# A new order of work for every engine in a four-stage transformer block on one core

## What is computed

```
x = x + tanh(g_xattn[0]) * L0_xattn(ctx, layernorm(x))      # queries from x, keys and values from [ctx | x], 8 heads of 64
x = x + tanh(g_ffn[0])   * L0_ffn(layernorm(x))             # quantised linear, depthwise conv, silu, quantised linear
x = x + tanh(g_xattn[1]) * L1_xattn(layernorm(x), ctx, ctx) # 16 heads of 8, rotary positions, 77 keys
x = x + tanh(g_ffn[1])   * L1_ffn(layernorm(x))             # 8 experts of 64, top 2, and a shared one
```

```
sim  = einsum('bhid,bhjd->bhij', q / scale, k)
attn = softmax(sim - max(sim))
out  = einsum('bhij,bhjd->bhid', attn, v) @ Wout
```

## Time and profile before

| | before |
|---|---|
| time, median of 3 runs | 274.52 us (273.43 to 274.93) |
| span of the profiled execution | 271.8 us |
| TensorE busy | 250.7 us (92%) |
| VectorE busy | 230.8 us (85%) |
| ScalarE busy | 184.1 us (68%) |
| GpSimd busy | 32.4 us (12%) |

### The profile page before, as it was taken

How to read it: one execution, slowest core, us unless ns; L and a number is a source line. 1 busy time by engine, 2 the same in 40 slices (tenths; PEclk the granted TensorE clock), 3 DMA queues, 4 the chain that set the end, 5 groups by cost and what they waited for, 6 DMA issues and landing times.

```text
span 271.8 us, 5455 instructions
## 1 busy us (share of the span) xinstructions
PE 250.7 (92%) x1772; PEld 185.5 (68%) x1772; DVE 230.8 (85%) x561; ACT 184.1 (68%) x462; POOL 32.4 (12%) x57
## 2 busy tenths in 40 slices
...
PEclk9999999999999999999999999999999999999999
...
DMA packets 8848, 10.70 MB, mean 39 GB/s; under 512 B 1115, under 2 KB 5877, under 8 KB 8821
## 3 DMA queue, kind: packets, MB, share of 16 engines
...
q10 hardware_dynamic: 1029, 0.65, 0.8%
...
## 4 chain that ended last, share of the span: by engine, by line
PE 62%; DVE 23%; issue 7%; ACT 6%; DMA 1%; DVEq 0%; ACTq 0%
PE slot L535 18%; PE slot L621 11%; PE slot L602 6%; PE slot L603 5%; PE slot L580 3%; PE slot L762 3%; PE slot L628 2%; PE slot L586 2%; DVE nm L1063 2%; ACT S L916 2%; DVE mx L1172 2%; ACT PR L842 2%; PE slot L756 2%; PE slot L592 1%; PE slot L713 1%
## 5 line engine op out<-in xcount | busy, mean ns | idle before, releaser
L842 ACT ACTIVATE PR<-slot,nm 128x589 f32<-128x589 f32 x64 | 47.6, 750 | 14.8 <-DVE nm L1063 12.5
L1063 DVE TENSOR_REDUCE nm<-slot 128x1 f32<-128x589 f32 x64 | 46.4, 763 | 3.6 <-PE slot L603 3.2
L535 PE MATMUL slot<-K,PR 128*128 128x128 f32 (+1 forms) x320 | 44.4, 278 | 1.7 <-ACT PR L842 1.5
L535 PEld LDWEIGHTS slot<-K,PR 128*128 128x128 f32 (+1 forms) x320 | 35.5, 142 | 12.3 <-ACT PR L842 10.2
L602 PE MATMUL slot<-KH,Q 128*128 128x296 f32 (+1 forms) x128 | 40.7, 336 | 0.8 <-DVE PT L779 0.4
L621 PE MATMUL slot<-PT,V 128*64 128x256 f32 (+1 forms) x320 | 38.1, 384 | 0.0
L603 PE MATMUL slot<-KL,Q 128*128 128x296 f32 (+1 forms) x128 | 36.1, 299 | 0.0
L621 PEld LDWEIGHTS slot<-PT,V 128*64 128x64 f32 (+1 forms) x320 | 21.6, 137 | 11.9 <-issue 2.7
L602 PEld LDWEIGHTS slot<-KH,Q 128*128 128x128 f32 x128 | 24.1, 188 | 5.6 <-issue 2.1
L777 ACT ACTIVATE PT<-slot 128x640 f32<-128x640 f32 x34 | 23.5, 705 | 6.4 <-PE slot L535 5.8
L779 DVE COPY PT<-slot 128x640 f32<-128x640 f32 x30 | 24.4, 820 | 2.6 <-PE slot L535 2.3
(11 more groups left out here) (170 smaller groups left out, 502.2 us busy)
## 6 DMA issues: line engine op xcount, KB each, us to landing
...
out<-X SPq DMA_DIRECT2D x8, 64.0 KB, 1.5
...
```

The costliest lines, as they stand in the source:

```text
L535: return pe.transpose(dst, src, ident[0:p, 0:p])
L842: act.activation(PR[:, s, :], W[:, K0:K0 + KEYS0], ACT.Exp, bias=nm0[:, s:s + 1], accum_out=sum0[:, b, p * 2 + f, t, e:e + 1]).then_inc(pr ...
L1063: dve.tensor_reduce(nm0[:, s:s + 1], W[:, K0:K0 + KEYS0], AX.X, ALU.max, negate=True).then_inc(max_ready, 1)
```

## The change

Only PLAN is replaced; no function changes. The words are the same but for the letters of the copies, and every engine's list has a new order. Of the 64 copies of u, 45 are ScalarE's and 19 VectorE's (34 and 30 before); of the 16 of a4, all 16 are ScalarE's (14 and 2 before); of the eight of f3, four each (six and two before); of the six of v, five are ScalarE's and one VectorE's, as before, but VectorE's is now the first of batch 0 (two chunks of 512 columns) and not the third (one chunk). Banks differ. s stands near the start, behind the first two rows of scores. f4 of tiles 2 and 3 of batch 0 comes before the last w of batch 1, and a4(0,0,0) too. m2 of tile 0 and 1, m3 of part 1 and m4 of tile 0, batch 0, come later against the last a4. The 86 turns stand at 11 places: 6 ahead of the first u, then 8 at the turn of a4(0,0,1), 3 and 7 ahead of f2(1,2) and f2(1,3), 26 and 8 ahead of a4(0,2,0)'s and a4(0,2,1)'s scores, 2, 3, 10, 7 and 6 at f3, a4(0,2,0)'s turn and f4 of batch 1. Behind f4(1,2) there is none. The lines cut here are of the same make.

```diff
 PLAN = """
-x0:F0 x0:A1 k:F2+8@2 x0:D2 q:F4 k:A1 k:F0 q:A1 k:D1 v:F6 x0:P2 k:A1 q:D1 v:F2 v:Ca k:D1 q:F5 v:Ca u:F6 x0:D3
-q:A1 u:F2 u:F0 u:D1 v:F4 u:D1 u:A1 u:D1 u:A1 u:B v:Cd u:A1 u:B u:Cd q:F4 u:Ca q:D1 u:F6 u:F2 u:D1 u:B u:D1
-q:F5 u:A1 u:Cd u:A1 u:B w:D0 s:D2 u:F0 w:P1 u:Ca u:B u:D1 u:F6 u:Ca u:D1 u:A1 u:F2 u:A1 u:B u:D1 q:A1 u:B
...
-f4:A1 u:B w:D0 u:D1 u:A1 w:P1 f4:B f3:F0 u:Cd u:A1 u:B f3:D1 w:F4 u:Ca f4:D2 f3:A1 f3:Ca f4:P2 u:F6 f4:D3
-w:A1 u:F0 w:D1 u:D1 a1:F5 o:F4 a1:A1 u:D1 u:A1 a1:P1 a2:F5 o:D1 u:A1 u:B a2:D1 o:F4 u:Ca u:B w:D0 o:D1 w:P1
...
-a1:A1 a4:A1 a2:F7 a1:P1 f1:D1 a2:D1 f2:F6 a4:A1 a4:B a4:D1 f2:A1 f2:F7 a4:D3 a4:Ca a4:B f2:A1 f2:D1 f2:F2
-f2:F3 a4:Ca f2:A1 a4:F0 f2:D1 f2:A1 f2:A2 f2:D1 a4:F6+8@6 f2:A2 a4:A1 f2:D1 f2:D2 a4:B+10@2 f2:D2 f2:A2
-a4:D1 f2:A2 a4:Ca a4:F2 f2:D2 a4:A1 f2:D2 a4:B+6@4 a4:D1 f3:F4 a4:Ca a4:D1 f3:F5 a4:A1 a4:F0 f3:D1 f3:D1
-f3:A1 a4:B a4:A1 f3:Cd f3:F4 a4:D3 f3:A1 a4:B a4:D3 a4:Ca f4:F5 f3:Ca a6:D0 f3:F6 f3:D1 a6:P1 f4:A1 f4:F7
...
-f4:B a2:D1 a4:B a4:Ca a6:D3 a4:F6+10@4 f4:D2 m1:F4 a4:F0 a4:D1 m1:A1 f4:P2 m3:F2 a4:D1 a4:A1 a4:F4 m3:D1
-a4:A1 f4:D3 a4:B+10@3 a4:D3 m3:A1 a4:B a4:Ca a4:D3 a1:F3 a4:Ca m2:F6 a4:D1 a1:A1 m3:D2 a1:P1 a4:F0 a4:A1
-m2:B a2:F3 a4:D1 m2:A1 a4:B m2:A2 m2:P1 a2:D1 a4:A1 a4:Ca a4:B+7@2 a6:D0 a4:F4 a4:D3 a6:P1 a4:Ca a6:F2 m2:D1
-a6:D0 a4:D1 a4:F0 m2:D2 a6:A1 a6:P1 a4:A1 a6:D1 a4:F6 a4:D1 a6:B a6:F3 a4:D1 a4:A1 a6:D2 a4:A1 a4:B a4:B
-a4:Cd a6:P2 a4:Cd a4:F4+5@2 a6:A1 a6:D3 a4:B a6:D1 m1:F2 a4:D3 a4:Ca m4:F0 a4:D1 a6:B m1:A1 m4:A1 m3:F2
-m2:F6 a6:D2 a4:A1 m4:B m2:A1 m2:P1 a4:D3 a4:B m4:D2 m2:B a6:P2 a6:D0 a4:Ca m3:D1 a6:P1 m2:F0 m2:A2 a6:D3
...
+x0:F4 x0:A1 k:F0 q:F6 k:A1 v:F4 q:A1 k:D1 q:D1 k:F2 k:A1 v:Cd v:F0 u:F6+6@4 v:Ca k:D1 u:F2 u:F4 u:F0 u:D1 u:A1 u:D1 u:B u:D1
+u:A1 u:D1 u:A1 u:B u:B u:Cd u:A1 u:Cd u:F6 u:Ca u:B u:F4 s:D2 u:D1 u:Ca v:F2 u:A1 s:F3 u:D1 s:D1 u:A1 q:F1 v:Ca u:B
+w:D0 u:B u:Ca u:F2 w:P1 k:F6 u:D1 u:Ca u:F4 q:A1 k:A1 q:D1 u:D1 u:A1 k:D1 w:F0 u:B u:A1 w:D0 u:B w:A1 u:Ca u:F6 w:D1
+u:Ca u:F2 u:F0 u:D1 u:A1 u:D1 u:D1 u:F4 u:B u:D1 u:A1 u:B u:A1 u:Cd u:Cd u:A1 u:B u:Cd u:F6 w:D0 u:B q:F2 q:A1 u:F0
...
+u:B u:B u:F2 u:Ca u:D1 f4:A1 a3:F4 f3:Ca w:P1 u:A1 f4:D3 a3:D1 w:F1 f4:B u:Ca f4:D2 u:B w:A1 a3:P1 u:Ca u:F6 w:D1 a1:F0 a1:A1
+u:F4 o:F2 u:D1 u:A1 f4:F1 a2:F3 u:D1 o:D1 u:B u:A1 f4:A1 f4:B w:D0 w:P1 u:Ca u:B o:F2 u:Ca a2:D1 f4:D2 o:D1 f4:P2 a4:F6 a4:D1
+w:F2 w:A1 f4:D3 n:P2 a3:F0 n:D3 w:D1 o:F2 a3:D1 o:D1 o:F5 a4:F2 o:D1 a4:D1 a4:A1 a4:B a4:F0 a4:Ca a4:A1 a1:F7 a1:A1 n:P2 a4:B+8@4 a4:D1
+a4:F6 n:D3 a2:F5 f1:F4 a4:A1 a4:D1 f1:A1 a4:Ca f1:D1 a4:D3 f2:F2 f2:A1 a2:D1 f2:F3 f2:A1 f2:D1 a4:B a4:Ca f2:A2 f2:D1 f2:F5+3@4 f2:D2 f2:F2+7@4 f2:A1
+a4:A1 f2:A1 f2:D1 f2:A2 a4:F4+26@0 a4:B f2:D2 f2:D1 f2:A2 a4:Ca a4:F6+8@0 a4:D1 f2:A2 f2:D2 a3:P1 a4:A1 f2:D2 a1:P1 a4:D1 f3:F2 f3:D1 f3:F1+2@0 f3:F3 a4:A1
+a4:B+3@0 a4:Ca f3:A1 a4:B f3:D1 f3:Cd f3:A1 f4:F4+10@0 f3:F5 f3:D1 f4:A1 f3:Ca f3:D1 f4:B f4:F1 f3:A1 f4:D2 f4:A1 a4:D3 a4:Ca f3:Ca f4:B+7@0 a4:F2 f4:F0
+f3:A1 a1:P1 f4:A1 f4:D2 f4:P2 a4:D1 f4:B+6@1 a1:P1 a6:D0 f4:D3 a4:F4 a6:P1 f3:Ca a4:A1 f4:F7 a1:F1 f4:D2 a6:F6 a4:D1 a1:A1 a2:F0 a4:D3 a4:B a6:A1
+a6:D1 f4:A1 a4:A1 f4:B a4:B a4:Ca a2:D1 f4:D2 a4:F2 a4:D1 a4:F0 f4:P2 a4:Ca a4:A1 a4:D3 a6:B a4:F4 a4:D1 f4:D3 a1:F7 a1:P1 a6:D2 a4:A1 a1:A1
+a4:B a4:Ca a4:D1 a4:B a6:D0 a4:Ca a4:F6 a2:F2 a4:D3 a4:D1 a6:P1 a4:A1 a6:P2 a6:F1 a4:B a6:D3 a4:A1 a4:B a6:A1 m1:F0 a4:Ca m1:A1 a2:D1 a4:D3
+a6:D1 a4:F4 a4:F2 m3:F0 a4:D1 a4:Ca a4:D1 a6:B a6:D0 a4:F6 a4:A1 a4:A1 a6:P1 a4:B a4:Ca a4:B a6:D2 m3:D1 a4:Ca m3:A1 a4:D1 a4:A1 a4:F4 m3:D2
+a6:F2 a6:P2 a6:A1 m2:F0 a4:D1 a6:D1 m2:A1 a6:D3 a4:B m2:B a4:A1 m1:F3 a4:D3 a4:Ca a4:D3 m2:A2 a6:B a4:B a6:D0 m2:F6 m2:P1 m2:D1 a4:Ca m2:B
+m1:A1 a6:P1 m2:A1 a6:D2 m2:A2 m3:F3 m2:D2 m2:P1 a6:F2 m4:F0 m2:F4 m2:D1 m2:B a6:P2 m3:D1 a6:D3 m3:A1 m3:D2 a6:A1 m4:A1 a6:D1 m2:A1 m2:D2 m4:B
...
 """
```

More of the change, by code:

```diff
@@ L107 @@
[L107 to L121, removed]
@@ L127 @@
-u:B u:Ca a3:F2 n:P2 u:Cd n:D3 w:F4 a3:D1 a3:F0 w:A1 w:D1 a3:P1 f4:F5 a3:D1 f4:F6 f4:A1 o:F7 f4:A1 o:F4 o:D1
-a3:P1 f4:B f4:B o:D1 a4:F2 f4:D2 a4:F0 n:P2 f4:D2 a4:F4 n:D3 f4:P2 f4:D3 f1:F6+22@6 a4:D1 a1:F7 f1:A1 a4:D1
-a1:A1 a4:A1 a2:F7 a1:P1 f1:D1 a2:D1 f2:F6 a4:A1 a4:B a4:D1 f2:A1 f2:F7 a4:D3 a4:Ca a4:B f2:A1 f2:D1 f2:F2
-f2:F3 a4:Ca f2:A1 a4:F0 f2:D1 f2:A1 f2:A2 f2:D1 a4:F6+8@6 f2:A2 a4:A1 f2:D1 f2:D2 a4:B+10@2 f2:D2 f2:A2
-a4:D1 f2:A2 a4:Ca a4:F2 f2:D2 a4:A1 f2:D2 a4:B+6@4 a4:D1 f3:F4 a4:Ca a4:D1 f3:F5 a4:A1 a4:F0 f3:D1 f3:D1
```

34 lines of the change are left out of this document (21 added, 13 removed).

## The result

| | before | after |
|---|---|---|
| time, median of 14 runs each | 274.61 us (273.43 to 275.24) | 272.94 us (270.21 to 276.37) |
| ratio, 95% interval | | 0.991 [0.988, 0.994] |
| span of the profiled execution | 271.8 us | 269.5 us |
| VectorE, ScalarE busy | 230.8, 184.1 us | 223.2, 190.5 us |

The account below looks back on a forecast made before the run. TensorE was taken to bound head and tail, VectorE the middle. Span 271.8 + 1.8 (head) - 7.5 (middle) + 3.4 - 0.75 (tail) = 268.8 us, 3.0 less, so time 274.5 - 3.0 = 271.5 us; range 268.0 to 275.5.

Parts of the forecast that it names:

- Middle: From w(1,3,1) to the last score maximum, VectorE-bound: 7.5 us shorter, including 1.9, 0.65 and 0.7 for words moved ahead.
- The rival that ScalarE becomes the wait: Middle: VectorE waits for ScalarE, 0.5 us at each of 12 exchanges, 6 us; median 277.4 us; chance 0.11.
- The clock's rival: Between f2(1,0) and f4(1,3): the clock falls in the stretch of turns, costing 4.3 us; 275.8 us; chance 0.07.
- Head: Start to w(1,3,1), TensorE-bound: w(1,3,1)'s product on VectorE comes 1.8 us later, 1.2 + 1.6 - 1.0.
- Term (a): Head, at w(0,0,0): TensorE waits 1.2 us for q(0,1)'s subtraction, queued on VectorE behind the chain of s.
- Term (b): Head: f4(0,2), f4(0,3) and a4(0,0,0)'s scores now precede w(1,3,1) on TensorE, 1.6 us more.
- term (c): Head: VectorE's relief, 4 us of words fewer, takes back 1.0 us of at most 2.6.
- rival 4: Head gains too: all 2.6 us of waits go and none shows at w(0,0,0); 268.7 us; chance 0.15.
- Tail: From a4(1,3,1) to the end, TensorE-bound: 2.65 us longer, 3.4 for words moved there less 0.75.
- rival 2: Between f2(1,0) and f4(1,3): the clock falls to 1.2 GHz in the stretch of turns; 275.8 us; chance 0.07.
- the step of the sum that took 0.75 back: Tail: a4(1,3,1)'s turn starts when its exponential ends, as the words in its way are gone, 0.75 us back.
- the 3.4 of the sum: Tail: TensorE words of m4, m3 and m2 come behind a4(1,3,1)'s turn, with the weights' rounding 3.4 us more.

Follow-up runs that it names:

- Experiment 12: e3_both with two VectorE words, f4(0,3):D3 and a4(0,0,0):D1, put back behind w(1,3,1):D1; 269.1 us, ratio 0.981 to the kernel before.
- 6: Kernel before up to w(1,3,1):F on TensorE, then every word not yet done in e3_both's order; 274.44 us, ratio 1.001 to the kernel before.
- 9: e3_both with the score copies of a4(1,2,0) and a4(1,2,1) given back from ScalarE to VectorE; 272.15 us, ratio 0.995 to the kernel before.
- e10: e3_both without the 26 and 8 identity turns ahead of the scores of a4(0,2,0) and a4(0,2,1); 271.24 us, ratio 0.987 to the kernel before.
- e3_both: Kernel after plus 22 turns where TensorE idles behind f4 of batch 1 and eight ahead of the first key projection; 268.59 us, ratio 0.980.
- e8_filled_f1: e3_both with f1(1)'s front moved ahead of a2(0,1)'s on TensorE, with 13 turns added; 268.98 us, ratio 0.980 to the kernel before.
- 4: Kernel before without its 32 identity turns at a4 of batch 1; 275.41 us, ratio 1.005 to the kernel before.
- e1_late_turns: Kernel after plus 22 turns where TensorE idles behind f4 of batch 1; 269.96 us, ratio 0.984 to the kernel before.

## Why the prediction came out as it did

**Middle, right: -8.0 measured, -7.5 predicted.** VectorE was busy 54.73 of 57.3 us, as full as before. Experiment 12 confirms the price of words moved ahead at about four fifths, 6 shows the condition (the head must take them in), 9 that putting two score copies back costs 3.4 and not 1.5, since a copy that is late makes TensorE and with it VectorE wait; what they gave in the change itself is not separated from the other words. The rival that ScalarE becomes the wait did not come: of VectorE's waits for it from 170 to 228 us the view of the waits after lists one, 0.2 us. The clock's rival was priced for this stretch and did not come at the turns either; e10 shows that they stood against it.

**Head, wrong by 2: -0.2 measured, +1.8 predicted.** Term (a) rested on a wrong reading. I gave w(0,0,0) two banks, of which one was q(0,1)'s; it takes one, whose former holder was u(0,0,0,1,1), so it waited for nothing:

```profile
29.37 0.41 PE L527 MATMUL slot<-K,REC 128*128 128x128 f32 x2
...
33.02 0.77 PE L527 MATMUL slot<-K,PR 128*128 128x128 f32 x5 [0.23 <-ACT PR L834]
34.63 0.37 PE L594 MATMUL slot<-KH,Q 128*128 128x296 f32 x1 [0.84 <-DMA KL<-KL]
```

The chain of s shows as the 0.23 at the next item. The 0.84 is the key copy of SyncE, which my sum held at nothing: issued behind the weight loads, which are still under way, it takes over three times as long to land as at other times; the wait was between 0 (e3_both) and 1.65 us (e8_filled_f1) in the kernels with this head. The issues of transfers after (count, size, median us to landing), from 22 to 26 us and over the span:

```profile
KL<-KL SPq DMA_DIRECT2D x2, 147.5 KB, 8.8
...
KL<-KL SPq DMA_DIRECT2D x16, 147.5 KB, 2.6
```

The first line is the pair of copies that u(0,1,0,0,0):F waits for, issued at 24 us.

So +1.1 came after all, by luck and elsewhere. Missing in the sum was also the later full rate at the start (u(0,0,0,0,0):F +0.7); part of it is chance, since the old order starts this word at 17.47 and 17.56 in experiments 4 and 6. Term (b) came as forecast, about 1.7 by the weights of the five words in the new trace. Against these 3.5 us stand -0.46 at w(1,3,1):F: of term (c) not 1.0 but 4.0 came back, more than the 2.6 of gaps I had counted. Where the full rate begins alike the gain is larger: w(1,3,1):F starts at 165.67 in e1_late_turns (full rate from 11.9 us), which has the head of the kernel after, and at 167.77 and 168.21 in experiments 4 and 6 (11.5 and 12.3), so the new head is 2.1 to 2.5 us earlier although it holds five words more. Where it comes from is not shown. From 88 to 128 us TensorE was busy 39.55 of 40 us before and 40.00 after, and the waits that the profile lists for it from 16 to 166 us fall from 2.3 to 1.3 us, which is too little. Records overlap by some 0.16 us, so a wait may cost more than the gap that it leaves; this is a guess. So the head went the way of rival 4, by more than the two profiles that I had compared show.

**Tail, wrong by 3.3: +5.9 measured, +2.65 predicted.** Some 2.1 us of this is the fall of the clock (41.8 against 39.7 in e1_late_turns, the only change being turns); the times differ by 1.9. That is rival 2's mechanism at another place: I looked where many turns stand, and it falls where none do. The rest, 1.2, is in the step of the sum that took 0.75 back: with the full clock (e1_late_turns) the last turn starts 3.96 us behind its maximum, where it took 3.25 before and was to take 2.5, held by a copy and a normalisation that end together, and by two words ahead. Behind that turn the words moved into the tail cost 3.1 us (35.8 against 32.7), near the 3.4 of the sum.

The two errors of opposite sign, 2.0 and 3.3, with 0.5 in the middle, leave 271.5 close to 271.86 (272.94 over all 14 runs). The total was nearer than its terms, and that is luck. One more reading was off: of the 2.7 us between the span and the time, which I took to lie around the span, only 1.8 do (271.27 us of time to 269.5 of span in the profiled execution after, and alike in the others); the other 0.9 is that the profiled execution of the kernel before was faster than its median.
